# Two AdaLN blocks on one core: stores of query parts reordered, a row-maximum step moved, and identity products put ahead of seven waits of TensorE

## What is computed

```python
h = layernorm(x) * (1 + ca) + sa
x = x + ga * attention(h)          # block 0: causal, 32 query heads of 16, 8 key and value heads
h = layernorm(x) * (1 + cb) + sb
x = x + gb * mlp0(h)               # relu^2 MLP 512->1024->512 plus a routed low-rank path (gate, top 2 of 8)
h = layernorm(x) * (1 + ca1) + sa1
x = x + ga1 * mixer(h)             # block 1: down to 128, hydra twice, up to 512
h = layernorm(x) * (1 + cb1) + sb1
x = x + gb1 * mlp1(h)              # silu(h w1) * (h w3), then w2; 512->1376->512, each with a rank-16 addition
```

## Time and profile before

| | |
|---|---|
| runs | 853.30, 854.83, 856.59 us; median 854.83 |
| profiled execution | 854.79 us, of which the span of its instructions is 853.0 |
| busy share of the span | PE 88%, PEld 52%, DVE 56%, ACT 37%, POOL 31% |
| chain that ended last | PE 67%, DVE 11%, issue 8%, POOL 8%, ACT 3%, DMA 2% |
| mean granted clock of PE | 0.944 |
| waits for DVE's `nm`, on PE | 11.2 us, 7 times |

### The profile page before, as it was taken

How to read it: one execution, slowest core, us unless ns; L and a number is a source line. 1 busy time by engine, 2 the same in 40 slices (tenths; PEclk the granted TensorE clock), 3 DMA queues, 4 the chain that set the end, 5 groups by cost and what they waited for, 6 DMA issues and landing times.

```text
span 853.0 us, 10154 instructions
## 1 busy us (share of the span) xinstructions
PE 751.9 (88%) x3710; PEld 444.2 (52%) x3710; DVE 477.2 (56%) x720; ACT 314.7 (37%) x528; POOL 265.9 (31%) x219
## 2 busy tenths in 40 slices
PE   5797983999999999879889999797778899997998
PEld 2343331333333333217658888543346688885886
DVE  3768761667776767306845637793687433336310
ACT  4211352566665656761315510244212322332100
POOL 0318547431312303151236513232223122222500
PEclk9997896999999999999989999998779899998999
DMA  9360623061321410212003300110320011111111
GB/s 323 129 122 2 146 65 83 1 146 44 68 84 27 110 64 1 91 38 62 0 27 112 97 1 1 52 41 1 48 63 29 25 50 49 49 39 36 61 62 38
DMA packets 24111, 53.00 MB, mean 62 GB/s; under 512 B 4252, under 2 KB 8100, under 8 KB 23044
## 3 DMA queue, kind: packets, MB, share of 16 engines
q1 hardware_dynamic: 24068, 52.44, 22.1%
HBM read 45.63 MB, written 6.60 MB: 61 GB/s over the span
## 4 chain that ended last, share of the span: by engine, by line
PE 67%; DVE 11%; issue 8%; POOL 8%; ACT 3%; DMA 2%; SPq 1%; ACTq 0%; POOLq 0%; DVEq 0%
PE ps L833 65%; DVE mxp L1688 2%; ACT pr L1374 2%; DVE xnb L1565 1%; DMA rq<-in_mask 1%; POOL wsum L2100 1%; PE ps L850 1%; PE ps L982 1%; POOL qacc L2070 1%; POOL qsw L2069 1%; POOL qacc L2073 1%; POOL qparts L2004 1%; DVE st L1543 1%; DVE arena L1572 1%; DVE dg L1912 1%
## 5 line engine op out<-in xcount | busy, mean ns | idle before, releaser
L833 PE MATMUL ps<-arena 128*128 128x512 f32 (+1 forms) x1416 | 333.6, 397 | 13.0 <-ACT full L1499 5.4
L833 PEld LDWEIGHTS ps<-arena 128*128 128x128 f32 (+1 forms) x1416 | 266.0, 189 | 74.7 <-DVE arena L1575 11.8
L1688 DVE TENSOR_REDUCE mxp<-ps 128x2 f32<-128x1024 f32 (+3 forms) x160 | 173.4, 1115 | 85.6 <-PE ps L833 69.2
L1374 ACT ACTIVATE pr<-ps 128x512 f32<-128x512 f32 x288 | 161.6, 596 | 118.8 <-PE ps L833 117.0
L833 PE MATMUL ps<-Qst,Kst 99*128 99x512 bf16 x288 | 106.1, 391 | 7.1 <-ACT pr L1374 4.2
L833 PE MATMUL ps<-Kst,Qst 96*128 96x512 bf16 (+3 forms) x384 | 102.6, 339 | 6.5 <-DVE mxp L1688 4.8
L833 PE MATMUL ps<-pr,vr 128*32 128x512 f32 x576 | 79.4, 624 | 0.7 <-ACT pr L1374 0.7
L833 PE MATMUL ps<-maskb,identb 128*128 128x128 bf16 (+1 forms) x320 | 75.3, 258 | 0.0
L833 PEld LDWEIGHTS ps<-Kst,Qst 96*128 96x128 bf16 x384 | 36.4, 100 | 73.1 <-DVE mxp L1688 27.5
L833 PEld LDWEIGHTS ps<-Qst,Kst 99*128 99x128 bf16 x288 | 27.3, 98 | 77.0 <-ACT pr L1374 58.4
L2191 POOL TENSOR_TENSOR arena<-raw,arena 128x1024 fp32r<-128x1024 f32 x11 | 26.6, 2418 | 85.8 <-ACT arena L1440 85.8
(11 more groups left out here) (190 smaller groups left out, 809.8 us busy)
## 6 DMA issues: line engine op xcount, KB each, us to landing
wmr<-in_wmr SPq DMA_DIRECT2D x8, 1280.0 KB, 6.4
raw<-in_w SPq DMA_DIRECT2D x16, 512.0 KB, 3.3
Qst<-q_parts SPq DMA_DIRECT2D x42, 128.0 KB
q_parts<-qparts SPq DMA_DIRECT2D x3, 768.0 KB, 8.5
x<-in_x SPq DMA_DIRECT2D x8, 256.0 KB, 5.9
wm<-in_wm SPq DMA_DIRECT2D x4, 512.0 KB, 7.1
raw<-in_up SPq DMA_DIRECT2D x8, 256.0 KB, 2.6
raw<-in_down SPq DMA_DIRECT2D x8, 256.0 KB, 2.7
```

The source lines that it names most:

```text
L833: return nc.tensor.matmul(outp, lhs, rhs, start=start, stop=stop, skip_group_check=True)
L1374: A(pr[:, k % PRING, :], ps[:, 4 + k % 2, :], ACT.Exp, scale=float(DH) ** -0.5).then_inc(exp_done, 1)
L1688: V.tensor_reduce(mxp[:, kh, g0:g0 + heads, i].rearrange("p (b e) -> p b e", e=per), units, AXX, ALU.max)\
```

## The change

Four things are changed.

1. On SP, `store_queries(1)` now stands ahead of the loop over the heads, and stores 2 and 3 behind the loads of heads 2 and 3, instead of each behind `head_dmas` and ahead of the loads.
2. On DVE, the wait for `part_q` 3 moves from the start of `head_body(1)` into `ctx_norm(0)`, two reductions later.
3. In `body_steps` the step `max` comes two transposed units later. DVE's own order stays; PE's changes.
4. `keep_warm(job, products)` waits for the job's bank and makes that many bf16 products of `identb` with `identb` repeated to 512 columns into it. The job's own first product overwrites them. It stands ahead of the waits for `ln_split(1, 0)` at the gate (14), for `dg` in the four `scale` steps (16, 9, 6, 4), for `xnb` in `ln_turn(3, 0)` (12), and for `ln_split(3, 0)` at the first `h1` (16): 77 products.

```diff
--- before.py
+++ after.py
@@ -127,6 +127,7 @@
 MIXER_POOL.remove(("out", 1, 1))
 MIXER_POOL.insert(MIXER_POOL.index(("up", 1, 0)), ("out", 1, 1))
 SPLIT_LNS = (1, 3)
+WARM_SCALE = (16, 9, 6, 4)
 
 
 def split_turn(L, hf):
@@ -337,7 +338,7 @@
     out, sofar = [], 0
     for what, d, s, cost in todo:
         step = sofar * NTU // max(total, 24000)
-        out.append((max(step, 3) if what == "ctx" else step, what, d, s))
+        out.append((max(step, 3) if what == "ctx" else step + 2 * (what == "max"), what, d, s))
         sofar += cost
     return out
 
@@ -742,11 +743,14 @@
                     sp.wait_ge(wsum_ready, h + 1)
                     sp.dma_start(wmr[:, :, :].rearrange("p c n -> p (c n)"), a["wmr"][h + 1]).then_inc(wmr_in, 16)
 
+            def store_queries(c):
+
+                sp.wait_ge(part_q, c)
+                sp.dma_start(qscr[c, :, :, :].rearrange("q p t -> p q t"), qparts[:, :, :]).then_inc(q_out, 16)
+
+            store_queries(1)
             for h in range(NKV):
                 head_dmas(h)
-                if h < 3:
-                    sp.wait_ge(part_q, h + 1)
-                    sp.dma_start(qscr[h + 1, :, :, :].rearrange("q p t -> p q t"), qparts[:, :, :]).then_inc(q_out, 16)
                 if h < NKV - 2:
 
                     sp.wait_ge(q_out, 16 * ((h + 2) // 2))
@@ -754,6 +758,8 @@
                         sp.wait_ge(t_full, h * NTU)
                     load_keys(h + 2, every, st_in[h + 2])
                     load_queries(h + 2, every, st_in[h + 2])
+                if h < 2:
+                    store_queries(h + 2)
 
             sp.wait_ge(modrow_out, 16 * NKV)
 
@@ -841,8 +847,16 @@
             def hilo(pair, f):
                 return f(pair[0]), f(pair[1])
 
-            def ln_turn(L, hf):
-
+            def keep_warm(job, products):
+
+
+                b = bank_of(pe, job)
+                for _ in range(products):
+                    mm(ps[:, b, :], identb[:, :], identb[:, :].unsqueeze(1).to_broadcast([P, 4, P]), True, True)
+
+            def ln_turn(L, hf, warm=0):
+
+                keep_warm(("ln", L, hf, 0), warm)
                 pe.wait_ge(ln_xn, 8 * L + 4 * hf + 4)
                 for c in range(KC):
                     b = bank_of(pe, ("ln", L, hf, c))
@@ -1066,6 +1080,7 @@
 
 
             for hf in range(2):
+                keep_warm(("gate", hf), 14 if hf == 0 else 0)
                 ln_split(pe, 1, hf)
                 weights(pe, "gate")
                 b = bank_of(pe, ("gate", hf))
@@ -1183,6 +1198,7 @@
                     last.then_inc(full_b[b], 1)
                 elif kind == "scale":
 
+                    keep_warm(("rbc", y, hf), WARM_SCALE[2 * y + hf])
                     pe.wait_ge(dg_ready, 2 * y + hf + 1)
                     b = bank_of(pe, ("rbc", y, hf))
                     mm(ps[:, b, :], ones[:, :], dg[:, :, :].rearrange("p t n -> p (t n)"), True, True)\
@@ -1193,7 +1209,7 @@
                         lora(("F", c), c)
                 elif kind == "up":
                     if hf:
-                        ln_turn(3, 0)
+                        ln_turn(3, 0, 12)
                     weights(pe, "wup")
                     pe.wait_ge(ho_ready, 2 + hf + 1)
                     for t in range(4 * hf, 4 * hf + 4):
@@ -1217,6 +1233,7 @@
                 mm(ps[:, b, :], Ast[:, 1024 + c * P:1024 + (c + 1) * P], Bst[:, 2 * HC1 * P:2 * HC1 * P + D], True, True)\
                     .then_inc(full_b[b], 1)
 
+            keep_warm(("h1", "F", 0, 0), 16)
             ln_split(pe, 3, 0)
             gated(("F", 0), ("w13", 0), 0, (0,))
             gated(("F", 1), ("w13", 1), 1, (0,))
@@ -1709,6 +1726,8 @@
 
             def ctx_norm(n):
 
+                if n == 0:
+                    dve.wait_ge(part_q, 3)
                 for b in range(2):
                     v = ps[:, 2 * b, :].rearrange("p (g i c) -> p g i c", g=G, c=32)
                     dve.wait_ge(s_full, ctx_at(n) + b + 1)
@@ -1744,8 +1763,6 @@
                 s_unit(1, s)
             swap_queries(3)
             for n in range(NKV - 1):
-                if n == 1:
-                    dve.wait_ge(part_q, 3)
                 head_body(n, True, n < NKV - 2, n > 0)
 
             dve.wait_ge(ga_in, 16)
```

## The result

The kernel after takes **834.37 us** (median; 833.72 to 835.15), the kernel before 855.71 in the same series (853.3 to 856.6). The ratio is 0.9755, with a 95% interval from 0.9731 to 0.978: 21.3 us, or 2.4%, faster. The forecast was 831.4 us with a range from 826.5 to 839.0, so the time came out 3.0 us above the forecast and inside the range.

The account below looks back on a forecast made before the run. TensorE, busy 88% of the span, was taken as the bound, with time only where it waits or runs at half clock. 854.8 less 22.8 (attention) and 0.6 (identity products) gave 831.4 us, range 826.5 to 839.

Parts of the forecast that it names:

- The stall from head 1 to head 2: Attention: interval between `nm` starts 19.15 us too long; reordered stores gain it, less 1.0 for POOL, net 18.1 us.
- the maximum's step: Attention, heads 2 to 6: taking `nm` two units later gains 0.75 us each, 3.75 in all; bounds 0.45 and 0.95.
- The rival of the in-order queue of SP: Store 2 ahead of head 1's rows of maxima holds up PE if part 2 is late; about 860 us; 3%.
- the rival by which head 1 keeps part of its stall: Another release comes late, so only 16.8 us plus 0.6 are gained; 837.4 us; 10%.
- POOL beside DVE's maxima: Head 1: POOL working until 119.9 slows DVE's maxima; loss taken as 1.0 us, bounds nothing and 2 us.
- The identity products: Gate, mixer and second MLP: 77 products cost 3.0 and 2.5 us and bring 6.1 by the clock; net -0.6 us.
- Behind the second and third `dg`: Mixer: clock kept up by products; of 2.1 us DVE allows 1.1 at the second, 2.8 come whole at the third.
- Behind the first `dg`: Mixer: 1.9 us stay idle behind the products, so 0.8 of the 1.7 us clock loss is counted as gained.
- The clock at waits that stay: Gate, second MLP, down: clock there depends on when waits fall; either sign, up to 3 us, taken as nothing.
- That the identity products don't hold the clock: Rival: 3.0 and 3.1 us are paid for products and nothing comes back; 838.1 us; 15%.
- That the wait for `nm` goes whole and POOL disturbs nobody: Rival, attention: 19.15 + 6 x 1.47 + 0.96 = 28.9 us gained; 825.3 us; 8%.
- That they overrun at half clock: Rival: identity products run at half clock and overrun their waits, costing 16.7 us; 848.7 us; 4%.

Follow-up runs that it names:

- doubled groups: Kernel after with 28 identity products at the gate instead of 14 and 32 ahead of `h1` instead of 16, mixer unchanged; 841.8 us.
- at the waits: Kernel after, mixer groups 23, 14, 9, 5, 22; gate and `h1` products moved to their second halves (22 and 24); 832.7 us.

## Why the prediction was right

**The stall from head 1 to head 2** was read rightly in its cause, and 53.84 - 35.87 = 17.97 us came against 18.1. That the two agree within 0.1 is in part luck. The 18.1 was worked out for the stores alone, against 34.69 us for a steady head, and the two runs without the step and the products show 53.84 - 37.39 = 16.45 and 53.84 - 37.29 = 16.55 (the 53.84 itself is one trace; the kernel with products alone had 52.61). With the maximum's step as well, the interval is 35.64 to 37.23 us in eight traces, and 35.87 is near the low end; of it, 35.87 - 34.10 - 1.05 (below) = 0.7 us are not accounted for. The cause is shown by three runs: the new order of the stores alone takes it away, the moved wait alone leaves it, and the maximum's step leaves it too. The rows behind it came as worked out: part 3 at 120.9 (119.9 forecast), store 1 out as soon as its data were there. One reading is to be corrected: the prediction has the store behind "the loads of the head". Of loads only that of the weights (`wmr`) stood ahead of it; what made the queue wait were the rows of maxima, and the later of the two stores, 13.6 us late, which it leaves out, is the one that made the 14.57 us. The rival of the in-order queue of SP fell with the same rows, since part 2 was stored at 98.67, far ahead of the point (about 127) at which it would have held anybody up. So did the rival by which head 1 keeps part of its stall. Its sum, 837.4, had dropped the 4.7 us of the maximum's step, which its own condition leaves alone; with them it is 832.7, which a time alone could not have told from the forecast.

**POOL beside DVE's maxima.** 1.0 us was taken, with bounds of 0 and 2. In head 1 the `nm` took 0.62 and the first cast 0.83 us, against 0.19 and 0.21 in head 2: 0.43 + 0.62 = 1.05 us. Each of the two ended with POOL's operation beside it (118.67 against 118.63, and 120.93 against 120.85), so each waited for the whole of it, as the rule has it that gave "near the upper bound, 2 us"; but only these two met one, and the upper bound was not reached.

**The maximum's step** was forecast at 0.75 us for each steady head and gave 0.59 (34.69 - 34.10), within its bounds of 0.45 and 0.95. The mechanism was the one described, the copy of `full` taking the place of `nm`: the rests are 0.38 us for ACT and 0.32 for DVE. For the interval from head 6 to 7 the forecast had 0.75 + 0.96 = 1.71 us, and 2.11 came. The runs with the maximum at its old place show how that is made up: an interval with a dip of the clock (granted 0.95 over it instead of 1.00) takes 36.21 us there instead of 34.69, so a dip costs 1.52, and the last interval takes 34.13 without one, which the step makes 33.54: 1.52 + 0.59 = 2.11. The dip had been mis-sized, since 34.69 was taken as the rule for an interval whose rule is 34.13. Attention in all, forecast 22.8: 0.1 less from head 1 to 2, 0.6 less in the four steady intervals, 0.4 more in the last, and 0.4 less from head 0 to 1 (38.54 us instead of 38.12; in the other kernels here 36.9 to 38.7, so no part of the change is to be seen in it). That makes the 22.0.

**The identity products** were forecast at -0.6 us in all. The medians with and without them differ by just that, but it is within the scatter and so luck, and the parts were met to a different degree:
- The price of a product, 0.217 us, was right (0.216 and 0.214 by the doubled groups), and so was the reading that the gate's 14 and the 16 at `h1` hide behind nothing. The groups cost 3.0 and 3.4 us where the stretch behind them runs alike; the kernel without the two lies 4.7 us below that with them. Forecast were 5.5.
- Behind the second and third `dg`: 15.63 - 14.53 = 1.10 and 16.33 - 13.56 = 2.77 us, forecast 1.1 and 2.8. The limit that was named for the second, DVE's own work ahead of `hof`, is seen as the new wait of 0.71 us at 587.39.
- Behind the first `dg` 0.8 us were forecast, as a share of 1.7, and nothing came. This is the term that was mis-sized, and a mean was the wrong form for it: the table above shows that it is all or nothing.
- From the transposes of `xnb` to the first `h1` it takes 10.18 us (7.49 before), where 1.1 us more had been forecast (2.5 paid, 1.4 gained) and 2.69 came. With the same products on the kernel before, whose clock did not fall there, that stretch is 8.50 us, the forecast 8.6. The 1.7 us between are the clock that fell at the 2.53 us left idle: the eight products that follow took 4.68 us instead of 3.60.
- The clock at waits that stay was taken as nothing, with up to 3 us either way. The stretches without added products came to 0.6 us less in all: the 36 products of the gate's second half took 9.79 us instead of 10.82 and the 24 of the second half of `h1` 7.24 instead of 8.07, while the 426 products of the first MLP that begin behind a wait of 1.61 us took 98.45 instead of 96.92, the granted clock of their first 10 us being 0.83 instead of 1.00.

**The sum.** The profiled execution took 835.15 us, 3.75 above the forecast: 0.8 are the attention, 1.8 the products (+1.2 us from the last maximum to the end instead of -0.6), and 1.2 the first maximum, which came later by scatter. The 1.8 are the 0.8 behind the first `dg` and 1.6 from `xnb` to `h1`, less the 0.6 at waits that stay. So the time came out near the forecast with two terms of the products too good by 2.4 us together. The median of the runs is 0.8 us below that execution.

**The rivals.** That the identity products don't hold the clock is refuted, by the windows above and even for transposes. (The prediction argued against it that nothing but products with the identity stood between 637.64 and the 48 products from 645.13. Eight products of `Wuo` stood there too, from 641.11 in 3.64 us, which is already full clock, so the clock had risen by their start and the argument stands.) That the wait for `nm` goes whole and POOL disturbs nobody is refuted by 0.59 us for a steady head instead of 1.47, and by the 1.05. That they overrun at half clock did not happen in the kernel after; it is what happened, by way of a bank, in the run "at the waits".

## What to carry to other kernels

A store that frees a buffer belongs on an in-order queue at the point where its data are ready, not behind transfers that wait for something later: here that alone was some 16 us, and the wait at which the loss showed (DVE's) was two engines away from it and needed no edit.

Filling that is to keep TensorE's clock up paid only inside a wait that was there anyway, and only where it wrote to a bank that had long been read. How full the wait has to be is known only by these traces: with 0.38 us or less left idle the clock never fell at the two places tabled above, with 1.86 to 2.83 left it fell in seven of nine cases, and 0.85 to 1.42 left at two others did no harm. The untouched 1.61 us in the first MLP made the clock fall in six of thirteen traces. Look for whom the wait is before choosing the bank: if the wait is for the bank itself, the filling lands behind it. Thirty products outside any wait cost 5 us here, and 64 inside three waits gained 6.

## What the runs showed of the hardware that was not expected

- One float32 transpose of 128x128 took 0.12 us (16 in 1.94) and a bf16 product of 512 columns 0.216, and groups of either kind that last equally long held the granted clock equally well (intervals of 14.54 and 13.56 us with both).
- In the attention, PE's regular wait of 1.47 us for `nm` now and then cost a dip of the clock, 1.52 us each: of the five intervals behind head 2, one or two had it in each of the four traces with the maximum at its old place and at the usual clock, and none had it in the nine traces with the later step. So the step gives more than the 0.59 us that a head shows.
- Beside an operation of POOL, DVE's `nm` took 0.62 to 1.16 us and a cast 0.83, where alone they take 0.19 and 0.21; in the two rows of the kernel after, each ended within 0.1 us of POOL's own.
